# A post-norm transformer layer, batch by batch: another order of the PSUM ring, of the fill work and of the second step

## The reference, cut to what matters

```
normed = rms_norm(x, gamma)
q, k, v = projections of normed, 8 heads of 16       # q scaled by 16 ** -0.5
q, k    = taylor(q), taylor(k)                       # 1, x, and all x_i x_j * 0.5 ** 0.5
state   = k^T v per head;  den = q . sum(k)
attn    = (q state / max(den, 1e-5)) @ w_out
x1      = layernorm(x + attn)
h = silu(x1 W1 * s1) * (x1 W2 * s2)                  # 128 -> 512
h = gelu(h H1 * hs1)                                 # 512 -> 512, exact gelu
h = gelu(h H2 * hs2)                                 # 512 -> 512
out = layernorm(x1 + (h W3 * s3))                    # 512 -> 128
```

## Time and profile before

| what | value |
|---|---|
| time, median of 3 runs (lowest, highest) | 576.32 us (576.15, 576.57) |
| the profiled execution's own time | 576.77 us |
| its span, first to last instruction | 575.0 us |
| busy: PE, DVE, ACT, POOL | 548.1, 458.6, 463.2, 164.4 us |
| PE weight loads (beside the matmuls) | 408.4 us |
| mean granted PE clock | 0.983 of full |

### The profile page before, as it was taken

How to read it: one execution, slowest core, us unless ns; L and a number is a source line. 1 busy time by engine, 2 the same in 40 slices (tenths; PEclk the granted TensorE clock), 3 DMA queues, 4 the chain that set the end, 5 groups by cost and what they waited for, 6 DMA issues and landing times.

```text
span 575.0 us, 11379 instructions
## 1 busy us (share of the span) xinstructions
PE 548.1 (95%) x3598; PEld 408.4 (71%) x3598; DVE 458.6 (80%) x976; ACT 463.2 (81%) x954; POOL 164.4 (29%) x246
## 2 busy tenths in 40 slices
PE   6869999999999999999999999999999999999994
PEld 3445877778687777768777776877777787786672
DVE  4775869878797988879798887979788797968664
ACT  4956797988879788887978888797888879787773
POOL 4541412323151332315133222413322241320000
PEclk9968999999999999999999999999999999999998
DMA  8000000000000000000000000000000000000000
GB/s 285 2 21 1 19 2 17 5 18 20 19 18 18 18 0 18 18 18 18 18 18 3 15 18 18 18 18 18 12 6 18 18 18 19 0 19 1 19 2 36
DMA packets 7366, 12.25 MB, mean 21 GB/s; under 512 B 816, under 2 KB 1840, under 8 KB 7344
## 3 DMA queue, kind: packets, MB, share of 16 engines
q1 hardware_dynamic: 7056, 11.86, 6.0%
q10 hardware_dynamic: 288, 0.10, 0.1%
HBM read 7.77 MB, written 4.19 MB: 21 GB/s over the span
## 4 chain that ended last, share of the span: by engine, by line
PE 69%; ACT 17%; issue 8%; DVE 5%; POOL 1%; DMA 1%; ACTq 0%; DVEq 0%; POOLq 0%
PE fps L422 20%; PE fps L423 20%; PE ring L359 6%; ACT phiT L644 5%; PE ring L389 5%; PE ring L339 4%; PE ring L313 4%; ACT fps L694 3%; ACT hid_hi L693 3%; PE ring L406 3%; PE ring L398 2%; PE ring L320 2%; ACT restq L649 2%; ACT x1T_hi L654 1%; PE fps L462 1%
## 5 line engine op out<-in xcount | busy, mean ns | idle before, releaser
L422 PE MATMUL fps<-hid_hi,w_hi 128*128 128x512 f32 x576 | 228.5, 397 | 2.3 <-DVE hid_lo L917 1.8
L423 PE MATMUL fps<-hid_lo,w_hi 128*128 128x512 f32 x576 | 226.9, 394 | 0.0
L422 PEld LDWEIGHTS fps<-hid_hi,w_hi 128*128 128x128 f32 x576 | 108.3, 188 | 29.3 <-DVE hid_lo L917 6.4
L693 ACT ACTIVATE hid_hi<-fps,col 128x512 fp32r<-128x512 f32 x128 | 90.5, 707 | 46.3 <-PE fps L423 45.9
L423 PEld LDWEIGHTS fps<-hid_lo,w_hi 128*128 128x128 f32 x576 | 108.4, 188 | 21.5
L917 DVE TENSOR_TENSOR hid_lo<-fps,hid_hi 128x512 fp32r<-128x512 f32 x128 | 88.1, 689 | 28.9 <-ACT fps L694 25.9
L644 ACT ACTIVATE phiT<-ring 128x512 f32<-128x512 f32 x128 | 78.6, 635 | 16.4 <-PE ring L339 16.2
L903 DVE SCALAR_TENSOR_TENSOR h<-fps,col,gate_zo 128x512 f32<-128x512 f32 x64 | 47.9, 748 | 49.8 <-ACT gate_zo L680 43.7
L694 ACT ACTIVATE fps<-fps,col 128x512 f32<-128x512 f32 x128 | 86.9, 679 | 0.0
L249 DVE TENSOR_TENSOR phi_k<-phi_k 128x896 f32<-128x896 f32 x64 | 73.0, 1145 | 1.4 <-ACT v_one L617 1.3
L339 PE MATMUL ring<-qT,sel 128*128 128x512 f32 x128 | 55.3, 441 | 7.7 <-ACT phiT L644 4.4
(11 more groups left out here) (98 smaller groups left out, 921.3 us busy)
## 6 DMA issues: line engine op xcount, KB each, us to landing
x_b<-in_x SPq DMA_DIRECT2D x16, 256.0 KB, 2.5
out<-gate_zo SPq DMA_DIRECT2D x16, 256.0 KB, 2.0
w_raw<-in_h SPq DMA_DIRECT2D x2, 1024.0 KB, 8.4
w_raw<-in_w SPq DMA_DIRECT2D x3, 256.0 KB, 4.0
sel_raw<-in_sel SPq DMA_DIRECT2D x1, 320.0 KB, 4.8
w_qkv_raw<-in_w_kv SPq DMA_DIRECT2D x1, 128.0 KB, 2.9
const<-in_consts ACTq DMA_DIRECT2D x1, 92.0 KB, 3.2
w_qkv_raw<-in_w_q SPq DMA_DIRECT2D x1, 64.0 KB, 2.9
```

Of the source, the lines that this page charges most:

```text
L422: nc.tensor.matmul(fps[:, bank, :], w_hi[:, o:o + P], hi, start=start, stop=False)
L423: return nc.tensor.matmul(fps[:, bank, :], w_hi[:, o:o + P], lo, start=False, stop=stop)
L693: nc.scalar.activation(hid[1 - layer][0][:, m, :], fps[:, bank, :], ACT.Gelu, scale=scale)
```

## The change

The ring's order becomes kv0 to kv3, qT, out, sq0 ..., sq6, state, sq7, with other banks from kv3 on. On PE kv2, kv3 and q are projected in the first half of layer two; the sums of q and rest move with them, and `state` follows `sq6`. ACT's and DVE's orders follow. The high half of a hidden tile gets a semaphore of its own; PE waits for the low half between the two matmuls. In steps 0 and 1: DVE squares `sq6` of batch 0 itself and rounds all three parts of the weights; ACT's sums of low bits move into step 1; PE does all projections, `sq0` to `sq2` and `rest0` before the branch, the transposes of x1 right after it, and layer one of step 2 follows at once, with `sq3` to `sq7`, `rest1` and `state` of batch 1 between and behind its first pairs. POOL does `k_small` for the second pair ahead of x1's inverse deviation.

```diff
 RING = (
     ("stateT", MIDDLE, 0), ("restT", MIDDLE, 1), ("xT", FRONT, 2), ("acc0", MIDDLE, 0), ("acc1", MIDDLE, 1),
-    ("kv0", FRONT, 3), ("kv1", FRONT, 2), ("kv2", FRONT, 3), ("out", MIDDLE, 0), ("qT", FRONT, 1), ("kv3", FRONT, 2),
-    ("sq0", FRONT, 3), ("sq1", FRONT, 0), ("rest0", FRONT, 2), ("sq2", FRONT, 1), ("sq3", FRONT, 3), ("sq4", FRONT, 0),
-    ("rest1", FRONT, 2), ("sq5", FRONT, 0), ("state", FRONT, 1), ("sq6", FRONT, 3), ("sq7", FRONT, 2))
+    ("kv0", FRONT, 3), ("kv1", FRONT, 2), ("kv2", FRONT, 3), ("kv3", FRONT, 2), ("qT", FRONT, 0), ("out", MIDDLE, 1),
+    ("sq0", FRONT, 2), ("sq1", FRONT, 1), ("rest0", FRONT, 3), ("sq2", FRONT, 0), ("sq3", FRONT, 2), ("sq4", FRONT, 1),
+    ("rest1", FRONT, 3), ("sq5", FRONT, 0), ("sq6", FRONT, 2), ("state", FRONT, 1), ("sq7", FRONT, 3))
...
+                nc.tensor.matmul(fps[:, bank, :], w[:, o:o + P], hi, start=start, stop=False)
+                if wait_lo is not None:
+                    pe.wait_ge(*wait_lo)
+                return nc.tensor.matmul(fps[:, bank, :], w[:, o:o + P], lo, start=False, stop=stop)
...
                     if m == 0 and made_by is None:
-                        pe.wait_ge(split_ready, KT * (t - 2) + k + 1)
+                        pe.wait_ge(hi_ready, KT * (t - 2) + k + 1)
+                        wait_lo = split_ready, KT * (t - 2) + k + 1
                     elif m == 0:
-                        pe.wait_ge(f_free[bank_of(FPS, f"{made_by}{k}")], read(FPS, t, f"{made_by}{k}"))
+                        pe.wait_ge(gelu_hi_ready, 2 * KT * (t - 2) + KT * ("two", "three").index(made_by) + k + 1)
+                        wait_lo = f_free[bank_of(FPS, f"{made_by}{k}")], read(FPS, t, f"{made_by}{k}")
...
             def second_step():
...
+                for j in range(NT):
+                    project_kv(1, j)
+                project_q(1)
+                pe.wait_ge(w_out_loaded, 16)
+                project_out(1)
+                sums_of_q(1, 0)
+                sums_of_q(1, 1)
+                rest_of_q(1, 0)
                 pe.wait_ge(lo_sums_ready, 3)
                 nc.tensor.matmul(fps[0:1, 3, 0:3], half_c, lo_sums[:, :], start=True, stop=True)\
                     .then_inc(lo_sums_added, 1)
+                sums_of_q(1, 2)
...
             with pe.If(lo_bits != 0):
-                second_step_sums()
+                transpose_x1(1, 0)
                 steps_from_2(pe, steps_with(True))
...
                 if middle:
-                    square_sums(t - 1, 7, 6)
+                    square_sums(t - 1, 7)
...
+            def square_sums(t, f):
+                bank = bank_of(RING, f"sq{f}")
+                dve.wait_ge(ring_full, written(RING, t, f"sq{f}"))
+                nc.vector.tensor_copy(phiT[:, f, :], ring[:, bank, :]).then_inc(sum_copied, 1)
+                dve.wait_ge(sum_copied, 1)
+                nc.vector.tensor_tensor(phiT[:, f, :], phiT[:, f, :], ring[:, bank, :], ALU.mult)\
+                    .then_inc(ring_free[bank], 1)
...
                 norm_scale(0, x1p, mv, rstd, mv_ready, rstd_ready, x1[0], x1_ready)
+                dve.wait_ge(lo_sums_added, 1)
+                nc.vector.tensor_reduce(lo_sum[:, :], fps[0:1, 3, 0:3], AX.X, ALU.add).then_inc(lo_sum_ready, 1)
+                phi_k_main(1, 1)
                 x1_lo(1)
```

More of the change, by code:

```diff
@@ L415, in transpose_x1, with product @@
                 mm.then_inc(f_full, 1)
-            def product(bank, o, hi, lo, start, stop, in_full):
+            def product(bank, o, hi, lo, start, stop, in_full, wait_lo=None):
+                w = w_raw if in_full else w_hi
                 if in_full:
[L420 to L423, removed]
+                    hi, lo = hi.bitcast(F32), lo.bitcast(F32)
+                nc.tensor.matmul(fps[:, bank, :], w[:, o:o + P], hi, start=start, stop=False)
+                if wait_lo is not None:
+                    pe.wait_ge(*wait_lo)
+                return nc.tensor.matmul(fps[:, bank, :], w[:, o:o + P], lo, start=False, stop=stop)
             def layer1(t, m, in_full):
@@ L692, in gelu @@
                 bank = bank_of(FPS, what)
-                nc.scalar.activation(hid[1 - layer][0][:, m, :], fps[:, bank, :], ACT.Gelu, scale=scale)
+                nc.scalar.activation(hid[1 - layer][0][:, m, :], fps[:, bank, :], ACT.Gelu, scale=scale)\
+                    .then_inc(gelu_hi_ready, 1)
                 nc.scalar.activation(fps[:, bank, :], fps[:, bank, :], ACT.Gelu, scale=scale)\
@@ L704, in step @@
                     silu(t, 0)
+                    square_sums(1, 3, 4)
+                    silu(t, 1)
+                    square_rest(1, 1)
+                    square_sums(1, 5, 6)
                 if middle:
@@ L711, in step @@
                 if middle:
-                    square_sums(t - 1, 7, 6)
-                if ffn:
+                    square_sums(t - 1, 7)
+                if ffn and not is_step(t, 2):
                     silu(t, 1)
@@ L752, in step @@
                 if is_step(t, 1):
-                    a, b = w_parts[0]
-                    nc.scalar.activation(w_hi[:, a:b], w_raw[:, a:b], ACT.Copy).then_inc(w_hi_ready[0], 1)
+                    weights_low_bits(2, 1)
+                if ffn:
+                    gelu(t, 0, 0)
+                    gelu(t, 0, 1)
+                if front and not is_step(t, 0):
+                    copy_q(t)
+                if is_step(t, 1):
+                    weights_low_bits(0, 2)
+                if ffn:
+                    gelu(t, 0, 2)
+                    gelu(t, 0, 3)
                 if front:
-                    square_sums(t, 0)
+                    square_sums(t, 0, 1)
                 if ffn:
@@ L779, in step @@
                     gelu(t, 1, 3)
-                if front:
+                if front and not is_step(t, 1):
                     square_rest(t, 1)
                     square_sums(t, 5)
-                if is_step(t, 0):
-                    weights_low_bits(1, 0)
+                if front and not is_step(t, 0) and not is_step(t, 1):
+                    square_sums(t, 6)
                 if middle:
@@ L943, in step @@
                     gelu_tile(t, 0, 1)
+                if front:
+                    q_lo(t)
+                if ffn:
+                    gelu_tile(t, 0, 2)
                 if middle:
                     sum_x1(t, 1 - par)
-                if ffn:
-                    gelu_tile(t, 0, 2)
-                if front:
-                    q_lo(t)
                 if ffn:
@@ L1099, in _ @@
             k_small(1, 0)
+            k_small(1, 1)
             inv_std(0, veps_ready, veps, rstd, rstd_ready)
-            k_small(1, 1)
             normed_x(2, 0)
```

100 lines of the change are left out of this document (40 added, 60 removed).

## The result

The changed kernel takes 568.84 us (median of 4 runs, 568.21 to 570.41), the kernel before on the same chip 576.45 (576.15 to 577.84): a ratio of 0.9867, 95% interval 0.9842 to 0.9893. In a second set of runs it took 568.79, ratio 0.9866 (0.9849 to 0.9884). The profiled execution took 568.82 with a span of 567.0, 8.0 less than the 575.0 of before.

The account below looks back on a forecast made before the run. PE was taken as the bound, busy 548.1 of 575.0 us. Full steps 6.8 plus tail 1.6 less head 0.8 gave 7.6 us of gain, so 568.7 us from the median 576.32; range 566.9 to 572.3.

Parts of the forecast that it names:

- Part 1: Full steps, new ring and order: 0.52 us a step, times 13, 6.8 us gained; bounds 4.6 to 7.4.
- The 0.47 at `sq5`: Full step: PE no longer waits at sq5 for sq4's square in a shared bank, 0.47 us a step gained.
- `b1`: Seventh matmul of the next step, waiting for ACT's copy of y: spare 0.14, cost 0 to 0.10, taken as 0.05.
- the 0.10 of k 3: Third layer, tile 0: the new order makes a late weight load come in time, 0.10 us a step gained.
- Part 2: Feed-forward, split wait: 192 added waits change nothing where PE is on time; where late, the high matmul runs beforehand.
- Rival E: Feed-forward steps: each of the 192 new waits costs 0.10, so slower, 587.9 us; chance 0.09.
- Part 3: Tail, steps 16 to 18: square 0.48, x1's sum 0.45, split waits 0.66, together 1.6 us gained; bounds 1.0 and 2.0.
- Part 4: Head, up to layer 1 of step 2: 0.8 us lost; bounds 1.6 lost and 2.4 gained.
- the 35.8: Head: the end of x1's scaling on DVE, put at 35.1 to 36.5 and taken as 35.8; before 37.91.
- the 1.2 of the four sums: Head: sq3, sq4, rest1 and sq5 still to do before the state is transposed, 1.2 us lost.
- rival C: Head: the branch is cheap, its record perhaps containing a queue wait; 3.2 us more gained, 565.5 us; chance 0.10.
- Rivals B and D: Full steps: part of the stall returns, 572.0 us, chance 0.13; or all 0.52 a step returns, 575.5, chance 0.08.

Follow-up runs that it names:

- experiment 1: Kernel before, with only the ring banks of sq5 and state exchanged, every order kept: 571.32 us, ratio 0.9902.
- experiment 5: Changed kernel with the banks of sq5 and state exchanged, so sq5 follows sq4 again: 579.36 us, ratio 1.005 to the kernel before.
- experiment 4: Changed kernel without the split wait, one wait per hidden tile ahead of both matmuls: 570.98 us, ratio 0.9908 to the kernel before.
- experiment 6: Kernel before with the split wait for high and low halves added and nothing else: 576.01 us, ratio 0.9989.
- Experiment 8: Changed kernel with ACT copying kv3 of batch 0 ahead of q in step 0: 568.10 us in one run.
- experiment 10: Changed kernel itself, unchanged, run again beside a version with a repaired head: 568.79 us (568.25 to 570.82).
- experiment 3: Changed kernel with the low-bit sums, their reduction, the load and the branch back where they were before: 563.58 us, ratio 0.9787 to the kernel before.

## Why the prediction was right, and where it was not

The forecast was 568.7 and the time 568.84. The mechanisms that it named came in the main, but two of its terms were off and cancelled: the full steps won more than their bounds allowed (8.6, bounds 4.6 to 7.4), the head lost more (2.17, bound 1.6). That the sum fits to 0.2 is luck.

*Part 1, 0.52 a step, 6.8.* Measured 0.65 a step, 8.6 between the marks. The 0.47 at `sq5` is right and is the banks' (experiments 1 and 5, from both sides). ACT did as worked out: from the first gelu of layer three to `sq4`'s square 275.25 - 269.29 = 5.96, the very number; the state's spare, put at 0.49, is 276.33 - 275.92 = 0.41. Three sizes were off. The sum left out that the wait at `sq5` also made the next weight load late (0.43 in the earlier trace rows); `sq6` to `state` is 0.33 now, so 0.10 more. `b1`, charged with 0.05, costs nothing: it follows at 0.23. And the 0.10 of k 3 was read from one step and put down for all thirteen. Before the change the interval is 0.30 to 0.33 in three of steps 2 to 15 and 0.22 to 0.26 in the others, as in this one:
```profile
236.75 0.39 PE L422 MATMUL fps<-hid_hi,w_hi 128*128 128x512 f32 x1
236.97 0.39 PE L423 MATMUL fps<-hid_lo,w_hi 128*128 128x512 f32 x1
```
On the mean it cost 0.03. Its cause was wrong too: the prediction gave it to the new order, but in the new order without the split (experiment 4) it is 0.11 a step, and it is the split that holds it at nothing. 0.47 + 0.10 + 0.03 = 0.60; the other 0.05 is spread over the rest of the step and was not taken apart.

*Part 2.* "Where PE is on time this changes nothing" stands: across the new waits PE takes 0.23 from a high matmul to its low one in the full steps, but for one place. Right behind the state product, in layer four, it is 0.34 in every step (278.54 to 278.88). That passes the 0.25 that the prediction named as a sign of being wrong, but the wait is not the cause: in experiment 4, which has none there, the same place takes 0.35 (278.69 to 279.04), and before the change the sum that stood behind the state product took 0.33 (213.80 to 214.13). Rival E (0.10 for each wait) is out. But PE was not on time everywhere, and so the split earned its 0.12 a step once the stall was gone. Before that it earned nothing in a full step (experiment 6).

The Trainium skill, "TensorE: Matmul & The Clock Gate", Part 2: What happens when you issue a matmul, says that PE pulls weight loads ahead of matmuls in flight, while matmuls keep their order. The rows agree: 0.23 where the load could run ahead, 0.30 to 0.34 where a semaphore came late.

*Part 3, 1.6.* Measured 1.57. Its inside was a little different: the split 0.82 to 0.88 (0.66 predicted), the square and x1's sum 0.69 together (0.93).

*Part 4, 0.8 lost.* This is the step that was mis-sized: 2.17 were lost. Layer one was put at 42.2 and came at 43.59, 1.39 late, of which 0.86 is the end of the scaling (36.66 for 35.8). The scaling itself fell from 2.06 to 1.11 as said. Ahead of it, x1's sum on DVE came 0.85 earlier than before (31.28 for 32.13; 1.09 counted from the first projection), where the 35.8 has 1.16 put down, so within the 0.5 to 1.8 of the prediction. What the prediction didn't see lies behind that sum. DVE's small instruction that makes `veps`, ahead of POOL's inverse deviation, took 0.72 in place of 0.17, and from it DVE works without a gap to the scaling, so 0.55 of the gain went there. With the 0.31 by which x1's sum fell short of 1.16 (0.24 of it the later start of this execution) that is the 0.86. The instruction now runs beside POOL's k_small of the second pair. DVE and POOL after the change, then DVE before:
```profile
31.28 0.69 DVE L869 TENSOR_TENSOR x1p<-x_b,ring 128x512 f32<-128x512 f32 x1
...
33.36 0.72 DVE L880 TENSOR_SCALAR veps<-mv 128x4 f32<-128x4 f32 x1
```
```profile
33.30 0.74 POOL L1081 TENSOR_TENSOR phi_k<-phi_k,k_mid 128x256 f32<-128x256 f32 x1
```
```profile
32.13 0.69 DVE L862 TENSOR_TENSOR x1p<-x_b,ring 128x512 f32<-128x512 f32 x1 [0.79 <-PE ring L406]
...
34.21 0.17 DVE L873 TENSOR_SCALAR veps<-mv 128x4 f32<-128x4 f32 x1
```
It is 0.71 or 0.72 in all seven profiles in which that k_small instruction covers it, and 0.17 in the three with POOL's old order (before, experiments 1 and 6). The prediction took the move of k_small as free but for its 0.95 of gain ("inv_std waits for the x1 sum anyway"); it gave 0.55 of it back, and that is the term that failed here. No run moved k_small alone, so this is argued from the traces.

The prediction also didn't follow the new table into step 0, where `sq0` sits in kv3's bank: PE's first sum moved from 13.96 to 15.21, the state from 18.59 to 19.41 (0.24 of both is the later start), and ACT then stood 1.35 idle before it could copy the state. Experiment 8 shows the bank as the cause, for 0.3 of layer one's time.

The other 0.53 of layer one's 1.39 is the way from the scaling's end to x1's transposes, with the reduction, the load and the branch (4.20 for 3.88), and from there to layer one (2.73 for 2.53, a number that ended with the low half and not with PE's start behind it).

From layer one to its third pair it took 9.53 for 8.03 of before, 1.5 lost. That equals the 1.2 of the four sums and the 0.3 of the state's copy together, but by chance: the four sums and `sq6`, which now stands ahead of the state, took 0.85 and 1.30 (45.43 to 46.28, 47.99 to 49.29), while the state product got shorter, 2.22 for 2.59, at a granted clock of 1.00 for 0.84.

The branch itself was right, and rival C out: it is the jump that costs, 3.3 to 3.8 us in every kernel where it is taken, 90 ns where it falls through; after the change it took its 3.37 although PE's last matmul ahead of it, at 36.09, was over. The Trainium skill, "Runtime: NRT & Kernel Launch", Instruction fetch mechanics, says that a taken branch out of the prefetched pages must fetch its target first; the rows agree with it. The Trainium skill, "Advanced Engine Details and Errata", Control Flow Timing, gives a compare-and-branch about 108 ns; that is near the 90 ns of the branch that isn't taken, while the loop branches of the earlier trace rows, 40 to 54 ns, agree less well than the prediction says.

Rivals B and D did not happen: in the full steps PE has no wait left in its list.

## What to carry to other kernels

Where banks are a ring, look at who was last in the bank of the tile that waits: exchanging two entries alone was worth 5.2 us here (3.4 of it in the full steps), and the change without its banks made the kernel slower. Look at a loss in more than one step before it is put down for all. Follow a new table through the first, shortened steps too, where other engines' orders differ, and ask of an instruction that is moved what runs beside it in its new place. A data-dependent branch belongs where its engine waits anyway: putting it back there was worth some 5 us more.

## What the runs showed of the hardware that was not expected

- A branch costs by whether it jumps: 90 ns not taken, 3285 to 3793 ns taken in the head in the profiles here, 4019 ns for the jump at the end.
- The spread between runs of one kernel goes with the mean granted clock, and the difference lies in the head. In experiment 10 the changed kernel's runs at 0.982 took 568.25 to 568.79, those at 0.976 and 0.977 took 570.82 and 570.43. Of its two profiled executions the one of 570.43 has the state product of step 1 at 50.91, the one of 568.82 at 49.29, 1.62 apart, and that of step 15 still 1.60 apart (507.36, 505.76). The granted clock of the first 30 us was 0.89 and 1.00. In the execution of 568.82 PE fell to 0.50 (1.2 GHz) for 13.65 us after a stretch of 4.10 in which it had worked 0.56; with the early branch (experiment 3) it fell too, after 5.00 us with 1.65 of work, but was 0.51 over 35 to 38 only and 1.00 over 40 to 50.
- A met wait between two matmuls costs nothing that shows. In the changed kernel, from high to low matmul, 171 of the 192 pairs with a wait take 0.230 on the mean and 368 of the 384 without one 0.231. The pairs left out are those of 0.28 and more, nearly all behind the state product, behind the output projection, or in the tail.
- A DVE instruction on 128x4 values took 0.17 us with POOL idle and 0.71 to 0.72 beside a POOL instruction of 0.74; the scaling of x1 took 1.11 and 2.06 in the same way.
